# Routed tiles of a mixture-of-experts layer: gate and up weights as the stationary operand, fetched per tile from DRAM

## What is computed

```python
def _swiglu(x, wg, wu, wd):
    return jax.nn.silu(x @ wg.T) * (x @ wu.T) @ wd.T
shared_out = _swiglu(x, shared_gate, shared_up, shared_down)
logits = x @ gate_w.T
top_id = jnp.argmax(logits, axis=-1)
score = jax.nn.sigmoid(jnp.max(logits, axis=-1))
xs = x * score[:, None]
def body(acc, ws):
    wg, wu, wd, e = ws
    xe = jnp.where((top_id == e)[:, None], xs, 0.0)
    return (acc + _swiglu(xe, wg, wu, wd), None)
...
x = x + 0.5 * _L0_ffn_ref(_layernorm(x, axis=-1), ...)
x = x + _L0_attn_ref(_layernorm(x, axis=-1), ...)
x = x + 0.5 * _L0_ffn_ref(_layernorm(x, axis=-1), ...)
```

## Time and profile before

| | us |
|---|---|
| median of 3 runs | 354.33 |
| lowest, highest | 351.35, 354.4 |
| the profiled execution | 352.44 |
| its span, first to last instruction | 350.6 |
| PE busy | 287.1 (82%) |
| DVE busy | 232.0 (66%) |
| ACT busy | 198.6 (57%) |
| POOL busy | 161.1 (46%) |

### The profile page before, as it was taken

The page is one execution under the profiler, slowest core; times in us unless marked ns, Lnnn a source line. Parts: engine busy times, 40 slices in busy tenths (PEclk is TensorE's granted clock), DMA queues, the critical chain, the costliest instruction groups (busy, mean ns, idle before and its releaser), DMA issues.

```text
span 350.6 us, 6524 instructions
## 1 busy us (share of the span) xinstructions
PE 287.1 (82%) x2124; PEld 181.0 (52%) x2146; DVE 232.0 (66%) x633; ACT 198.6 (57%) x440; POOL 161.1 (46%) x295
## 2 busy tenths in 40 slices
PE   0799959999145579999999999998999897999940
PEld 0765536666013235565656555555485565566630
DVE  6648814343165988898989899997966686334323
ACT  1254215454214578989898989897857531455410
POOL 2405788766334635253535264541210675256550
PEclk9999999999755999999999999999998999999995
DMA  7992136111310000000000000000000013511118
GB/s 205 169 328 94 53 91 132 53 47 37 107 43 0 2 0 4 0 3 2 0 2 3 0 3 2 2 1 3 2 0 3 23 55 85 142 47 37 39 46 239
DMA packets 24272, 18.42 MB, mean 53 GB/s; under 512 B 4944, under 2 KB 22608, under 8 KB 23984
## 3 DMA queue, kind: packets, MB, share of 16 engines
q1 hardware_dynamic: 21744, 12.88, 14.9%
q0 software_dynamic: 2496, 5.13, 4.5%
HBM read 10.30 MB, written 7.71 MB: 51 GB/s over the span
## 4 chain that ended last, share of the span: by engine, by line
PE 50%; DVE 27%; DMA 6%; issue 6%; POOL 5%; ACT 4%; SPq 1%; POOLq 0%; another core or an unknown queue 0%; DVEq 0%; ACTq 0%
PE bank L931 40%; DVE negmax L801 11%; PE bank L1098 3%; DVE qT L794 3%; PE bank L1060 3%; DVE xn L612 2%; DMA xs<-y_by_token 2%; DVE rs L818 1%; PE bank L1046 1%; PE bank L940 1%; DMA y_by_token<-ys,xg 1%; DMA x<-in_x 1%; DVE stats L622 1%; ACT kT L542 1%; DVE sh L719 1%
## 5 line engine op out<-in xcount | busy, mean ns | idle before, releaser
L801 DVE TENSOR_REDUCE negmax<-bank 128x2 f32<-128x512 f32 x128 | 83.5, 682 | 5.7 <-PE bank L931 4.1
L535 ACT ACTIVATE probs<-bank 128x512 f32<-128x512 f32 x128 | 71.8, 603 | 16.2 <-PE bank L931 15.8
L332 POOL DMA_INDIRECT y_by_token<-ys,xg x46 | 44.7, 972 | 32.5 <-issue 22.9
L766 DVE TENSOR_TENSOR rh<-rsg,bank 128x256 f32<-128x256 f32 x46 | 19.4, 421 | 47.5 <-ACT rsg L513 47.5
L931 PE MATMUL bank<-qT,kT 128*128 128x256 bf16 x256 | 49.1, 276 | 1.7 <-ACT qT L551 0.7
L323 POOL DMA_INDIRECT xs_sorted<-xs,slot x32 | 32.2, 1006 | 39.5 <-ACT xs L467 16.4
L931 PE MATMUL bank<-rgu,xgT 128*128 x92 | 47.2, 596 | 0.7 <-ACT xgT L505 0.7
L931 PE MATMUL bank<-kT,qT 128*128 128x512 bf16 x106 | 40.3, 380 | 5.0 <-DVE negmax L801 3.6
L513 ACT ACTIVATE rsg<-bank 128x256 f32<-128x256 f32 x46 | 17.7, 385 | 36.9 <-PE bank L931 36.9
L931 PE MATMUL bank<-probs,vx 128*32 128x256 f32 x512 | 35.0, 393 | 0.0
L542 ACT COPY kT<-bank 64x1024 bf16<-64x1024 bf16 x32 | 32.1, 1004 | 5.0 <-PE bank L1098 4.2
(11 more groups left out here) (114 smaller groups left out, 493.2 us busy)
## 6 DMA issues: line engine op xcount, KB each, us to landing
rgu<-in_rgu SPq DMA_DIRECT2D x1, 2048.0 KB, 20.1
xs<-y_by_token SPq DMA_DIRECT2D x8, 256.0 KB, 3.6
xg<-xs_sorted SPq DMA_DIRECT2D x6, 258.0 KB, 4.4
xs_sorted<-xg SPq DMA_DIRECT2D x1, 1483.5 KB, 16.2
x<-in_x SPq DMA_DIRECT2D x4, 256.0 KB, 4.8
rdn<-in_rdn SPq DMA_DIRECT2D x1, 1024.0 KB, 16.2
out_x<-x SPq DMA_DIRECT2D x4, 256.0 KB, 2.6
xg<-xs_sorted SPq DMA_DIRECT2D x4, 193.5 KB, 3.7
```

The costliest lines, as they stand in the source:

```text
L332: g.indirect_dma_start(y_dram, bass.IndirectOffsetOnAxis(ap=xg[:, j, D:ROW].bitcast(U32), axis=0), ys[:, j, :], None, bounds_check=N + SLO ...
L535: a.activation(probs[:, h % 8, :], stbank[st_bank(i, h)][:], ACT.Exp, scale=float(DH) ** -0.5).then_inc(exp_done, 1)
L766: v_.tensor_tensor(rh[:, 1 - u, :], rsg[:, 1 - u, :], gu_bank[1 - u][:, F:2 * F], ALU.mult).then_inc(rh_ready, 1)
L801: v_.tensor_reduce(negmax[:, w, t, h0 + 2 * pair:h0 + 2 * pair + 2], sbank[k % 2][:].rearrange("p (a s) -> p a s", a=2), AX.X, ALU.max, ne ...
```

## The change

The gate and up weights become the stationary operand, in four blocks of 128 columns, and the 128 tokens the moving one. The result is then already turned (hidden unit on the partition), gate in one bank and up in another, so the two transposes of `rh`, ACT's copy to `rhT` and the buffer `rh` go; DVE's product is written as `rhT`, and the down matmuls of tile j move from turn j + 1 into turn j. `rgu` holds eight tiles' weights instead of eight experts': SP fetches the 256 KB of each of the 23 tiles, 46 loads in all, by the expert's number, which it must first load into registers. Four of the loads stand ahead of the first `xg` load, four between the first and the second, and the others behind the last `xg` load (in the first layer behind the write of `spare`). PE waits for a semaphore of the tile's buffer; SP waits for PE (`up_filled`) before it fills a buffer again.

```diff
+WEIGHTS = 8
-        rgu = sb("rgu", [D, E * 2 * F], F32)
+        rgu = sb("rgu", [D, WEIGHTS, 2 * F], F32)
-            sp.dma_start(rgu[:], rgu_in).then_inc(rw_loaded, 16)
+            expert_regs = [sp.alloc_register(f"sp_expert{k}") for k in range(SLOT_TILES)]
             for n in range(2):
+                sp.wait_ge(expert_ready, n + 1)
+                sp.load(expert_regs, expert[0:1, :])
+                experts = [nc.sync.snap(r_, min_val=0, max_val=E - 1) for r_ in expert_regs]
+                def load_gate_up(j):
+                    g = n * SLOT_TILES + j
+                    if g >= WEIGHTS:
+                        sp.wait_ge(up_filled, g - WEIGHTS + 1)
+                    sp.dma_start(rgu[:, g % WEIGHTS, :], rgu_in[:, bass.ds(experts[j] * (2 * F), 2 * F)]).then_inc(gu_loaded[g % WEIGHTS], 16)
+                for j in range(4):
+                    load_gate_up(j)
                 for k, (j0, j1) in enumerate(LOADS):
                     if k == 0:
                         sp.wait_ge(scattered[0], 16 * FIRST * (n + 1))
                     if k == 1:
+                        for j in range(4, WEIGHTS):
+                            load_gate_up(j)
                         sp.wait_ge(scattered[1], 16 * (TILES - FIRST) * (n + 1))
                     sp.dma_start(xg[:, j0:j1, :], xs_slots[:, j0:j1, :]).then_inc(xg_loaded[k], 16)
...
+                for j in range(WEIGHTS, SLOT_TILES):
+                    load_gate_up(j)
# ACT, turn j
-                        act.wait_ge(gu_filled, r + j + 2)
+                        act.wait_ge(g_filled, r + j + 2)
-                        act.wait_ge(hT_filled, r + j + 1)
-                        a.copy(rhT[:, u, :, :].rearrange("p k s -> p (k s)"), hT_bank[u][:, 0:2 * P]).then_inc(hT_copied, 1)
# DVE, turn j
                         dve.wait_ge(rsilu, r + j + 2)
+                        dve.wait_ge(up_filled, r + j + 2)
-                        v_.tensor_tensor(rh[:, 1 - u, :], rsg[:, 1 - u, :], gu_bank[1 - u][:, F:2 * F], ALU.mult).then_inc(rh_ready, 1)
+                        v_.tensor_tensor(rhT[:, 1 - u, :], rsg[:, 1 - u, :], hT_bank[1 - u][:, 0:F], ALU.mult).then_inc(hT_ready, 1)
# PE, turn j
-                        mm(gu_bank[1 - u][:], xgT[:, 1 - u, :], rgu[:, bass.ds(experts[j + 1] * (2 * F), 2 * F)]).then_inc(gu_filled, 1)
+                        g = r + j + 1
+                        pe.wait_ge(gu_loaded[g % WEIGHTS], 16 * (g // WEIGHTS + 1))
+                        for k in range(4):
+                            ins = mm((gu_bank, hT_bank)[k // 2][1 - u][:, k % 2 * P:(k % 2 + 1) * P], rgu[:, g % WEIGHTS, k * P:(k + 1) * P], xgT[:, 1 - u, :])
+                            if k == 1:
+                                ins.then_inc(g_filled, 1)
+                        ins.then_inc(up_filled, 1)
-                        for k in range(2):
-                            ins = t_.transpose(hT_bank[u][:, k * P:(k + 1) * P], rh[:, u, k * P:(k + 1) * P], ident)
+                            ins = mm(ry_bank[u][:, 0:D], rhT[:, u, k * P:(k + 1) * P], rdn[:, bass.ds(experts[j] * (2 * D) + k * D, D)], start=(k == 0), stop=(k == 1))
```

More of the change, by code:

```diff
@@ L127, in build @@
         rsg = sb("rsg", [P, 2, F], F32)
-        rh = sb("rh", [P, 2, F], F32)
-        rhT = sb("rhT", [P, 2, 2, P], F32)
+        rhT = sb("rhT", [P, 2, F], F32)
         ys = sb("ys", [P, SLOT_TILES, D], F32)
@@ L184, in build @@
         xg_loaded = sems("xg_loaded", len(LOADS))
-        gT_filled, gT_copied, gu_filled, rsilu, rh_ready = (sem(n) for n in ("gT_filled", "gT_copied", "gu_filled", "rsilu", "rh_ready"))
-        hT_filled, hT_copied, ry_filled, ys_ready = (sem(n) for n in ("hT_filled", "hT_copied", "ry_filled", "ys_ready"))
+        gT_filled, gT_copied, g_filled, up_filled, rsilu, hT_ready = (
+            sem(n) for n in ("gT_filled", "gT_copied", "g_filled", "up_filled", "rsilu", "hT_ready"))
+        ry_filled, ys_ready = sem("ry_filled"), sem("ys_ready")
+        gu_loaded = sems("gu_loaded", WEIGHTS)
         y_scattered, y_loaded = sem("y_scattered"), sems("y_loaded", CHUNKS)
@@ L1037, in ffn @@
                 if n == 0:
-                    pe.wait_ge(rw_loaded, 32)
+                    pe.wait_ge(rw_loaded, 16)
                 def turn_g(j):
@@ L1057, in turn @@
                     if has(0):
-                        pe.wait_ge(rh_ready, r + j + 1)
+                        pe.wait_ge(hT_ready, r + j + 1)
+                        if r + j >= 2:
+                            pe.wait_ge(ys_ready, r + j - 1)
                         for k in range(2):
-                            ins = t_.transpose(hT_bank[u][:, k * P:(k + 1) * P], rh[:, u, k * P:(k + 1) * P], ident)
[L1061 to L1066, removed]
-                        for k in range(2):
-                            ins = mm(ry_bank[v][:, 0:D], rhT[:, v, k, :], rdn[:, bass.ds(experts[j - 1] * (2 * D) + k * D, D)], start=(k == 0), stop=(k == 1))
+                            ins = mm(ry_bank[u][:, 0:D], rhT[:, u, k * P:(k + 1) * P], rdn[:, bass.ds(experts[j] * (2 * D) + k * D, D)], start=(k == 0), stop=(k == 1))
                         ins.then_inc(ry_filled, 1)
@@ L1243, in _ @@
             pe.wait_ge(aw_loaded, 32)
-            for s_ in (gT_copied, rh_ready, hT_copied, ys_ready):
+            for s_ in (gT_copied, hT_ready, ys_ready):
                 pe.wait_ge(s_, SLOT_TILES)
```

9 lines of the change are left out of this document (3 added, 6 removed).

## The result

| | before | after |
|---|---|---|
| median of 4 runs, us | 354.2 | 362.55 |
| lowest, highest | 351.35, 354.4 | 360.9, 363.28 |
| ratio, 95% interval | | 1.0248, 1.0185 to 1.0312 |
| the profiled execution | 352.44 | 362.85 |
| its span | 350.6 | 361.1 |

The change makes the kernel 2.5% slower, 1.5 us above the upper end of my range. The profiled executions lie 10.4 apart and not 8.4, since before's is at the low end of its runs and after's at the high end of its own. In 13 of the 18 runs of experiments the kernel before itself took 366 to 382 us (a ratio is there taken against the lower of these, near 370), in 5 the 354 of above; sizes are taken from those five unless the text says otherwise.

What follows compares the result with a forecast made beforehand. It took PE to bound the routed part. First layer 1.9 + 1.3 - 4.0 = -0.8, second 4.5 - 4.0 = +0.5, together -0.3: median 354.0, range 349.8 to 361 (the forecast case alone 351.5 to 357.5).

Steps and rivals of the forecast that it cites:

- PE's turn 1.635 to 1.44: PE's routed loop: two transposes go, 0.22 less; eight gate and up passes take 0.89 against 0.86.
- 4.0 less per layer from the first transposes: Routed part of each layer: 4.0 less on PE, 0.3 less in the tail, 0.3 swallowed by waits for the product.
- POOL's floor: First layer's scatters of results on POOL: 59.45 + 22 x 1.275 = 87.5, capping any gain there at 3.1.
- SP's registers and issues: SP's queue before the first tokens: register load 2.5 or 2.2, steps 0.6, four weight issues 2.3.
- some queueing behind 1 MB of weights ... I take 0.4: First token load behind four weight loads: 0.4 to 1.5 of delay, taken as 0.4, beyond 3.85 to the first transposes.
- The clock: Rival: PE's clock falls in gaps of 4.3 and 4.4, about 2.0 lost per gap; 356, or 358 to 361; chance 0.2.
- Tile 8 waits 1.3, 0 to 4.5: First layer: PE waits 1.3 for tile 8's weights, issued behind the token landings and `spare`; bounds 0 and 4.5.
- "Nothing" for the 2 MB load that goes: Start of the kernel: dropping the 2 MB load changes nothing, as it landed long before the routed part.
- The weight stream sets the pace: Rival: weight loads slower than 1.44 us per 256 KB, below 182 GB/s, pace the turns; 362, chance 0.1.
- the estimate with the fixed cost: Weight loads: 2 us fixed per DMA, unoverlapped, makes 2.6 per tile, 35 more; chance within the stream rival's 0.1.
- PE's turn doesn't shrink: Rival: eight separate weight loads don't hide on PE, a turn of 2.1; 373, chance 0.03.
- the four stretches that are the change's: Numbers to first transposes, +1.9 and +4.5; first transposes to last scatter, -2.7 and -4.0, by layer.

Runs made afterwards that it cites:

- experiment 1: Changed kernel's compute alone, all weights resident, SP fetching nothing, a fixed expert per tile: 346.38 against 354.48 for the kernel before; 1.0215 and 1.0211 where that took about 370.
- experiment 6: experiment 5 plus four useless matmuls before each layer's first transposes: 353.81 against 354.29 for the kernel before, ratio 1.0001.
- experiment 7: experiment 5 with two weight loads ahead of the first layer's first tokens, tiles 6 to 11 spread between later token loads: 355.28 against 354.25 for the kernel before.
- experiment 5: Changed kernel with the first token load ahead of all weights, six weights before the other token loads, six behind: 353.15 against 354.29 for the kernel before.
- experiment 4: Changed kernel with useless matmuls, six before each layer's first transposes, four before tile 8: 389.88; kernel before 372.06, changed kernel beside it 387.75.
- experiment 2: Kernel before, its arithmetic kept, with eight weight buffers and the change's 46 loads in SP's order: ratios 1.0362, 1.0323 and 1.0234 (379.97 against 371.31).

## Why the prediction was wrong, step by step

- **PE's turn 1.635 to 1.44**: right (1.45 in after and in experiment 1). The eight weight loads were hidden as in the earlier trace rows.
- **4.0 less per layer from the first transposes**: right in the second layer where nothing disturbs it, 4.0 in experiments 1 and 6 (both 37.2). The first layer gains 2.3 in experiment 1. I had worked out that POOL's floor caps the gain there at 3.1; the rest is the slow turns, which the sum had nowhere, since the gap of before had not brought them.
- **SP's registers and issues**: right. I gave 5.4 and 5.1 from the numbers to the issue of the first tokens; it took 5.0 and 4.7 (44.87 and 304.31). Four issues took 1.9, not 2.3.
- **"some queueing behind 1 MB of weights ... I take 0.4"**: this is the first step that failed. PE started 6.2 after the issue of the tokens in both layers, not 3.85 + 0.4: 2.4 of queueing, outside my 0.4 to 1.5. The bound took 275 to 388 GB/s from the earlier trace rows. In the first layer's windows from 46 to 50 the DMA is full (share 0.90 and 1.04) at 253 and 290, so four loads take 3.6 to 4.1, less 1.9 of issuing 1.7 to 2.2, an estimate, near the 2.4. But in the second layer 336 GB/s in 306:308 gives only 1.2 by the same sum, and the tokens came as late. A rate times the bytes ahead doesn't explain it, the less as two loads ahead cost as much as four (experiment 7). That the loads ahead are the cause is shown by experiment 5 in the first layer: with none ahead and six behind, PE starts 4.1 after the issue of the tokens, in place of 6.2. How they come to cost 2 us isn't shown.
- **The clock.** This is the second step that failed, and the larger: the sum had it at nothing, with the fall as a rival at 0.2. It fell in both gaps, at 2.8 after the last matmul, while my own forecast gaps were 4.3 and 4.4. So it wasn't the missing 2 us of queueing that made it fall: by these windows it would have fallen in gaps as long as forecast, too. The condition that I set, a gap of about 4 us, came from two falls in before, and experiment 1 has one behind 2.24. The price per fall was right (about 2.0 forecast): 1.6 behind the gap in each layer of after, by the start of the third gate and up block in the first (4.76 against 3.18) and by the stretch in the second (38.8 against 37.2). But experiment 1 loses 1.7 in the first layer without any longer gap, so the first of these can't be put down to the late tokens.
- **Tile 8 waits 1.3, 0 to 4.5**: it waited 3.3, inside the bounds by luck. `spare` was issued at 59.64 (59.0 forecast). The weights behind it landed 7.70 after their issue, where I gave 4.8 to 6.9 (59.5 to 64.3 or 66.4); it was only because PE itself wanted them 1.7 later than forecast (64.73 for 63.0) that the wait stayed below 4.5. The Trainium skill, DMA: Bandwidth & Descriptors, section "Queues, rings and completion order", has the descriptors of an issuer taken in ring order. The trace agrees: `spare` landed 6.7 after its issue, at 66.3, and the weights behind it at 67.9, the longest landing of that layer's 23; in the second layer the four loads, the tokens and the fifth load landed in the order of their issue, between 306.1 and 311.2. What I left out is that behind this wait, too, the clock is down: 1.7 more (68.02 to 72.62). The first layer of after is then 37.2 + 1.6 + 3.3 + 1.7 = 43.8, against 43.9 measured, each part read from its own rows.
- **Not forecast**: the last scatter of tokens, which isn't in SP's queue at all, landed 6.34 after its start in place of 2.3 to 3.6 (experiment 5 had 6.11 with six weight loads moving, experiment 1 2.28 with none). It delayed the later tokens, `spare` and so tile 8.
- **"Nothing" for the 2 MB load that goes**: right, experiment 1 has it and isn't late.
- **The weight stream sets the pace** (0.1): refuted for after, no wait for weights from tile 9 on at 224 GB/s. The loads overlapped, landing in a median of 3.7 against a turn of 1.45; they weren't paid one after the other, as the estimate with the fixed cost supposed. The Trainium skill has the advice of 1 MiB in the section "Bandwidth" of the same page, but the fixed cost of about 2 us in "Anatomy of one DMA — SWDGE (gpsimd) path", for DMAs that GpSimd issues; these were SP's. **PE's turn doesn't shrink**: refuted.

In sum: -0.3 forecast for the four stretches that are the change's, +9.9 in the profiles. Of the 10.2 between, 3.1 are the later tokens (1.6 and 1.5), 2.0 the wait at tile 8 beyond the 1.3, and 4.9 the slow turns behind the three gaps (1.6 + 1.7 + 1.6); 0.2 is left. These rest on single profiles. No run shows that the 4.9 can be had back: experiment 4, the one direct test of the clock, showed that it can be held, at a price that was higher.

**What stays open.** Experiments 5 to 7 bring back 7 to 9 of the 16 us that the fetching costs, and none reaches the 346 of experiment 1. Where the rest of it goes is read from the profiles (waits of 3.6 and 2.4 for weights, a scatter that landed after 6.1, the clock at 0.50 in 52:54) but no run removed these without adding another. Blocks of resident weights addressed by a register weren't tried.

## What to carry to other kernels

Read the moment at which a new stream starts, not only its rate: 46 loads of 256 KB fitted beside the work with 0.73 of the DMA in use, but the tokens that everybody waited for, now behind the load of the numbers and the first 1 MB, came 3.5 and 6.0 later, more than the 8 us that the shorter turns could give. Put the load on the path first in its queue, and count the other queues' transfers too. Price the slow turns behind a gap in the sum itself and not as a rival of small chance. Here they came to 4.9 us, more than any other term, and a gap that had none behind it in the kernel before (2.41) was no promise for the next kernel (2.24 in experiment 1).

## What the runs showed that I hadn't expected

Beside the kernel before at 354 the compute part alone was 2.4% faster, beside it at 370 it was 2.1% slower. It isn't a matter of one chip against another as far as the record's chip numbers go: 0, 1 and 3 stand with both. In the profile of experiment 1's second run, at 376.5, DVE stands still for nothing that the profile names, three times while POOL scatters tokens (DVE group of the page: busy us, mean ns, idle before and releasers; then a row of the timeline):

```profile
L722 DVE SCALAR_TENSOR_TENSOR x<-bank,x 128x512 f32<-128x512 f32 x8 | 5.5, 692 | 26.2 <-remote 17.5 <-PE bank L928 8.0 <-issue 0.7
```

```profile
308.73 0.69 DVE L722 SCALAR_TENSOR_TENSOR x<-bank,x 128x512 f32<-128x512 f32 x1 [8.48 <-remote]
```

17.5 us in all, with PE idle 8.83 behind the longest. The same wait is in every profile taken beside 370, 8 to 19 us in all, and in none taken beside 354. What makes DVE stand there isn't settled, and so experiments 2 and 4, which ran only beside 370, say less than the others.

A load of 322 KB landed in 6.2 us behind 1 MB, and a scatter on another queue, which takes 2.3 alone, in 6.3 beside it.
